# A planner that counts slow TensorE stretches and breaks up runs of row-maximum products and geometric scores

## What is computed

```python
q, k, v = heads(xn @ Wq), heads(xn @ Wk), heads(xn @ Wv)   # rope on q and k
scores = jnp.where(causal, jnp.einsum('bhtd,bhsd->bhts', q, k) * scale, NEG)
out = jax.nn.softmax(scores, axis=-1) @ v
geo = jnp.where(causal, qp[..., :, None] * kp[..., None, :], NEG)
geo_out = jax.nn.softmax(geo, axis=-1) @ v
out = out + scales * (geo_out - out)
x = x + out @ Wo + ffn(xn)    # top-102 of 1024 hidden units, ternary weights
```

## Time and profile before

| | us |
|---|---|
| median of three runs | 769.25 (768.81 to 769.69) |
| the profiled execution | 764.82 |
| its span, from the first to the last instruction | 762.7 |
| PE busy in it | 703.0 (92%) |
| DVE, ACT, POOL busy | 495.1, 449.3, 225.2 |
| mean granted TensorE clock | 0.924 of full speed |

### The profile page before, as it was taken

One profiled execution on the slowest core, in us unless ns is written; L12 is line 12 of the kernel. 1 busy time (PEld: TensorE's weight loads), 2 busy tenths in 40 slices (PEclk: granted clock), 3 DMA queues, 4 the chain that ended last, 5 costly groups with the idle time before them and its releaser, 6 DMA issues.

```text
span 762.7 us, 12315 instructions
## 1 busy us (share of the span) xinstructions
PE 703.0 (92%) x4424; PEld 328.5 (43%) x4424; DVE 495.1 (65%) x973; ACT 449.3 (59%) x733; POOL 225.2 (30%) x304
## 2 busy tenths in 40 slices
PE   4799898999799999998999999999999999998993
PEld 2443443434444442343344444464444465454532
DVE  5855987476568665667685876876567757467602
ACT  5434444444674533367554443679989998977550
POOL 4332336203222120133100121224432334266332
PEclk9866987989999998988999999999989999999997
DMA  8485000002700000052000000010000000000000
GB/s 244 171 229 138 10 8 1 28 1 63 206 9 2 1 1 1 3 135 62 1 6 1 1 1 1 10 33 31 15 28 29 23 22 29 9 22 8 1 1 28
DMA packets 26162, 30.74 MB, mean 40 GB/s; under 512 B 7089, under 2 KB 21297, under 8 KB 25714
## 3 DMA queue, kind: packets, MB, share of 16 engines
q1 hardware_dynamic: 24178, 29.38, 13.5%
q10 hardware_dynamic: 1920, 0.54, 0.3%
HBM read 17.72 MB, written 11.53 MB: 38 GB/s over the span
## 4 chain that ended last, share of the span: by engine, by line
PE 74%; DVE 9%; ACT 5%; issue 4%; DMA 3%; SPq 1%; POOL 1%; ACTq 0%; DVEq 0%; POOLq 0%
PE acc L1432 17%; PE acc L1425 16%; PE side L1324 11%; PE scores L1407 8%; PE scores L1411 4%; ACT probs L899 3%; DVE piece_max L1133 3%; PE side L1361 2%; PE side L1303 2%; PE side L1378 2%; PE side L1386 2%; PE side L1379 2%; PE side L1369 2%; PE side L1362 2%; DVE side L1136 1%
## 5 line engine op out<-in xcount | busy, mean ns | idle before, releaser
L899 ACT ACTIVATE probs<-scores 128x1024 f32<-128x1024 f32 (+3 forms) x320 | 270.3, 892 | 239.4 <-PE acc L1432 195.8
L1133 DVE TENSOR_REDUCE piece_max<-side 128x1 f32<-128x512 f32 x190 | 126.3, 686 | 76.2 <-PE side L1324 74.5
L1425 PE MATMUL acc<-probs,v_nat 128*32 128x512 f32 (+3 forms) x1280 | 161.6, 579 | 2.3 <-POOL probs L756 1.5
L1432 PE MATMUL acc<-probs,ones_all 128*32 128x512 f32 (+3 forms) x1280 | 158.6, 569 | 0.0
L1324 PE MATMUL side<-k_stack,q_stack 96*128 96x512 f32 (+3 forms) x315 | 125.0, 452 | 9.9 <-DVE piece_max L1133 2.8
L756 POOL TENSOR_SCALAR_AFFINE_SELECT probs<-probs 128x256 f32<-128x256 f32 x128 | 55.3, 439 | 238.0 <-ACT probs L899 236.6
L1324 PEld LDWEIGHTS side<-k_stack,q_stack 96*128 96x128 f32 x315 | 56.9, 200 | 104.8 <-issue 48.5
L1407 PE MATMUL scores<-q_stack,k_stack 98*128 98x512 f32 (+3 forms) x320 | 91.8, 392 | 4.2 <-ACT probs L899 4.0
L1136 DVE CUSTOM_DVE_ANT_0 side<-side,tail_mask 128x256 f32<-128x256 f32 (+3 forms) x125 | 61.3, 497 | 23.6 <-PE side L1324 23.0
L1425 PEld LDWEIGHTS acc<-probs,v_nat 128*32 128x32 f32 x1280 | 37.4, 115 | 80.1 <-issue 68.1
L1159 DVE RECIPROCAL d_raw<-d_raw 128x512 f32<-128x512 f32 x16 | 53.5, 3347 | 27.5 <-ACT o_raw L912 27.5
(11 more groups left out here) (163 smaller groups left out, 900.1 us busy)
## 6 DMA issues: line engine op xcount, KB each, us to landing
q_stack<-q_parked SPq DMA_DIRECT2D x12, 512.0 KB, 7.1
q_parked<-turned SPq DMA_DIRECT2D x8, 512.0 KB, 3.0
res<-in_L_attn_x_dram SPq DMA_DIRECT2D x4, 512.0 KB, 6.3
x_parked<-xn SPq DMA_DIRECT2D x4, 512.0 KB, 2.9
xT_parked<-xnT SPq DMA_DIRECT2D x4, 512.0 KB, 2.7
xz<-xT_parked SPq DMA_DIRECT2D x16, 128.0 KB, 2.5
xb<-x_parked SPq DMA_DIRECT2D x16, 128.0 KB, 2.0
out_dram<-res SPq DMA_DIRECT2D x16, 128.0 KB, 1.7
```

The lines of the kernel that those rows point to most:

```text
L899: nc.scalar.activation(probs[:, slot % 2, pair, :, off:], scores[:, pair, :, off:], ACT.Exp, scale=ATT_SCALE if kind == 0 else 1.0).then_i ...
L1133: free(nc.vector.tensor_reduce(piece_max[:, h, p:p + 1], pt, AX.X, ALU.max), ("S",) + a)
L1425: nc.tensor.matmul(acc[D * h:D * h + D, 0, off:], v_nat[:, j, g], probs[:, slot_no[a] % 2, h // 2, h % 2, off:], start=(j == 0), stop=(j = ...
L1432: last = nc.tensor.matmul(acc[D * h:D * h + D, 1, off:], ones[:, 0:D], probs[:, slot_no[a] % 2, h // 2, h % 2, off:], start=(j == 0), stop ...
```

## The change

The planner gets two additions. First, TensorE's clock in the plan no longer advances by an operation's length alone. `array` splits time into stretches of a fixed length, adds up in each the work done, weighted by kind (`WEIGHTS`: 0.72 for `S`, 0.77 for the usual scores, 0.14 for geometric ones, 0.06 for `gx`, 1 for the rest), and lets the next stretch run at half speed where that sum is under `ENOUGH`. These are numbers of the code, no measurements. Second, `thin` names the kinds geometric scores, `S`, `gx`, `found` and `wsum`; `idle_work` counts the time since the last operation of another kind. Where a thin operation would take it over `LIMIT` (1200 ns), another kind is taken if one can start within `PATIENCE` (900 ns) of it. No instruction is added or taken away on any engine, and none changes in size; only the orders change, and with them the banks.

```diff
--- before.py
+++ after.py
@@ -46,6 +46,13 @@
            "xnT_park": 3500, "khi_park": 2200, "klo_park": 2200, "hi_park": 3500, "lo_park": 3500, "stack_hi": 6000,
            "stack_lo": 4500, "xz_in": 2300, "xb_in": 2300}
 STAT_RANK = 3
+WINDOW = 3413.3
+PHASE = 0.0
+ENOUGH = 1500.0
+FULL = 1.0
+WEIGHTS = {"S": 0.72, "score0": 0.77, "score1": 0.14, "gx": 0.06, "found": 0.0, "wsum": 0.0}
+LIMIT = 1200
+PATIENCE = 900
 LEAD = 0.02
 REACH = 0.85
 Z_RANK = 11
@@ -262,8 +269,31 @@
         resting = at < len(keys) and any(d not in done for d in op[keys[at]][2])
         return range(BANKS + 2 * PAIRS) if key[1] == "S" and resting else range(BANKS)
 
+    worked = {}
+
+    def speed(n):
+        return 1.0 if worked.get(n - 1, 0.0) >= ENOUGH else 0.5
+
+    def array(key, at, ns):
+        weight = WEIGHTS.get(key[1] if key[0] == "unit" else key[0] + str(key[3]) if key[0] == "score" else key[0], 1.0)
+        left_ = ns
+        while left_ > 0:
+            n = int((at - PHASE) // WINDOW)
+            v = speed(n)
+            part = min(left_, (PHASE + (n + 1) * WINDOW - at) * v)
+            worked[n] = worked.get(n, 0.0) + part / v * weight * FULL
+            left_ -= part
+            at += part / v
+            if part < 1e-6:
+                at += 1e-3
+        return at
+
     clock = {e: 0.0 for e in ("pe", "dve", "act", "pool", "sp")}
+    def thin(key):
+        return key[0] == "score" and key[3] == 1 or key[0] == "unit" and key[1] in ("S", "gx", "found", "wsum")
+
     mode = "full"
+    idle_work = 0.0
     heads = {q: 0 for q in queue}
     plan = {e: [] for e in clock}
     landing = LANDING
@@ -308,7 +338,12 @@
         first = min(b[0] for b in best)
         close = [b for b in best if b[0] <= first + SLACK and b[3] == min(best)[3]]
         start, rank, key, eng, flow, ns, m = min(close, key=lambda b: (b[1], b[0]))
+        if eng == "pe" and thin(key) and idle_work + ns > LIMIT:
+            full_ = [b for b in best if b[3] == "pe" and not thin(b[2]) and b[0] <= start + PATIENCE]
+            if full_:
+                start, rank, key, eng, flow, ns, m = min(full_, key=lambda b: (b[0], b[1]))
         if eng == "pe":
+            idle_work = idle_work + ns + start - clock[eng] if thin(key) else 0.0
             mode = m
             if key[0] == "unit":
                 i = min((i for i in banks_for(key) if free_from(i) is not None), key=free_from)
@@ -317,7 +352,10 @@
             if key[0] == "score":
                 for i in range(2):
                     holds[BANKS + 2 * key[5] + i] = key
-        clock[eng] = start + ns
+        if eng == "pe":
+            clock[eng] = array(key, start, ns)
+        else:
+            clock[eng] = start + ns
         done[key] = clock[eng] + landing.get(key[0], 0)
         plan[eng].append(key)
         heads[(eng, flow)] += 1
```

## The result

| | before | after |
|---|---|---|
| median of 13 runs, us | 768.27 (761.70 to 773.25) | 776.29 (771.08 to 777.66) |
| profiled execution, us | 764.82 | 776.06 |
| its span | 762.7 | 774.0 |
| PE busy | 703.0 | 700.8 |
| span less PE busy | 59.7 | 73.2 |

The changed kernel is slower by 1%: ratio 1.0107, 95% interval 1.0080 to 1.0135. 774.8 was forecast, in a range of 758 to 787.

A forecast was written before the change was run, and what follows sets the result against it. The prediction took PE, busy 92% of the span, as the bound: its work, low clock and waits. Terms -11 + 3.6 - 2 + 5.5 + 2 + 6.5 + 1 = +5.6 us gave a median of 774.8 us, range 758 to 787.

The forecast's parts named there:

- The clock, -11: Behind 85 us: half-clock stretches behind thin runs go, gaining 11 us, ends 5 and 16.
- the seven stretches: Half-clock stretches at 120 to 482 us behind row-maximum products and geometric scores; 32.60 us of busy PE, all to go.
- The prediction's rival on the other side: Whole kernel: clock gain larger than the stalls, low stretch at 51.73 us also halved; 760 us, chance 0.34.
- Changes of neighbour, +3.6: PE's order throughout: 36 more borders between value steps and other kinds at 0.1 us each, +3.6 us.
- Small waits, -2: PE ahead of usual scores: alternating scores and values leave ACT more time for exponentials, -2 us, ends -4 and +1.
- Chunk 0, +5.5: From `mT` to first usual scores: reciprocal ahead of `m` on DVE makes PE wait 7.5 instead of 1.65 us.
- Chunk 2, +2: From `gx` to first `S`: PE waits 7.0 instead of 4.9 us, for the stack; +2 us, ends 0 and +4.
- Chunk 3, +6.5: From `gx` to first `S`: 7.1 us of work, PE waits 8.5 instead of 2.1 us; ends +3 and +8.5.
- Chunk 1, +1: Rope transposes now come soon after `gx` of chunk 1; +1 us, ends 0 and +2.5.
- those for right: 100-490 us: no full-load low stretches behind thin work; chunk 3 first-`S` wait 4 us or more; chunk 0 distance some 9 us.
- those for wrong: Chunk 3 first `S` unwaited or under 14 us after `gx`; clock near 0.924; exponential waits growing in last third.
- The rival with pauses alone as the cause of the low clock: Whole kernel: no low stretch goes, borders and stalls stay, +17 us; 786 us, chance 0.06.

The follow-up runs named there:

- the one from 79 us: Changed kernel with both additions acting only from the planner's 79 us on; 767.75 us, ratio 0.9984 to the kernel before.
- dense piece: Changed kernel with one unit of rope transposes near 72 us done five times over, same result; 779.86 us, ratio 1.0133 to the kernel before.
- the clock model with the right landings: Changed kernel with the limit out of reach and stack landings planned at 9.5 and 8.6 us; 769.14 us, ratio 1.0000 to the kernel before.
- right landings: Changed kernel with the planner's stack landings set to 9.5 and 8.6 us instead of 6 and 4.5; 760.44 us, ratio 0.9904 to the kernel before.
- the limit from 79 us: Changed kernel with the clock model throughout but the limit only from the planner's 79 us on; 770.71 us, ratio 1.0038 to the kernel before.
- the reciprocal moved: Kernel with landings 9.5 and 8.6 us, chunk 0's second geometric reciprocal put behind `m` and five reductions on DVE; 760.99 us, ratio 0.9895.
- the moved reciprocal: Changed kernel, old landings, chunk 0's second geometric reciprocal put behind `m` and the five reductions that follow on DVE; 779.85 us, ratio 1.0142.

## Why the prediction was right, and where it was not

The forecast was +5.6 us; the medians of 13 runs differ by 8.0, the profiled executions by 11.2. By the steps of the prediction:

- **The clock, -11: in effect -1.** Its first half held in the main. Of the seven stretches two have a successor, with 6.83 + 10.13 = 16.96 us of busy PE instead of 32.60 in the seven. In all, PE's busy time at half clock behind chunk 0's scores fell by 16.4 us, and that is -7.7 of the -11, inside the ends of 5 and 16. What failed is that the term was summed over the seven stretches behind 85 us as if the order ahead of them stayed as it was. Ahead of the scores of chunk 0 the clock cost 6.7 us more, by one execution of each kernel. The changed kernel and its copies with the same order on PE there have 39.2 to 43.9 us of busy time at half clock, the kernel before and the one from 79 us 29.7 to 35.8; so the cost lies between 1.6 and 6.7 us. The prediction's rival on the other side had even priced that place as a gain (-4.7), "since value steps now come between its thin runs earlier". The reverse was measured. From 66 to 84 us value steps come one and two at a time between `S`, scores and transposes, and the clock stayed at half; the first three in a row (84.94 to 89.44) are followed by full clock at 90.11, and in the other kernel one dense piece brought it back at once. The reading that fits is that breaking up thin runs with single value steps also breaks up the runs of value steps, and that it is these that bring the clock back. The dense piece supports it, but no run here puts the value steps of this stretch together and keeps the rest, so it is argued and not shown. The kernels with the limit from the start and the old landings have 50.6 to 56.2 us at half clock ahead of chunk 0's scores (limit alone 53.3, the changed kernel 52.9, and its edited copies but for the dense one, which has 43.1); those without the limit there have 34.1 to 41.0 (before and the clock model alone 34.1, both from 79 us and the clock model with the right landings 37.5, the limit from 79 us 41.0). With the right landings it is 38.0 in spite of the limit, and 34.8 with the reciprocal moved, so the limit is not a sufficient cause.
- **Changes of neighbour, +3.6: about 0.** PE's busy time from 30 us to the last `sum`, less 47% of that at half clock, is 679.09 - 46.5 = 632.6 before and 678.16 - 45.5 = 632.7 after. The 36 more borders left no trace in these sums. The price of the way back was taken as 0.1 us without a row; whether that or the price of leaving the value steps failed is not shown.
- **Small waits, -2: 0.** For exponentials PE waited 4.0 + 3.0 us before and 5.0 + 1.9 after; for the cuts of the triangle 1.5 and 4.1. So the step that failed is that scores and values that alternate more leave ACT more time: the wait that the term was about grew by 1.0 us. The wait for the triangle's cut, which comes behind ACT on the same path, grew by 2.6 and had no term. In the last third (500 us on) the waits for exponentials grew from 2.3 to 3.5 us and those for cuts from 1.0 to 2.7: the growth that the prediction named as left out.
- **Chunk 0, +5.5: +2.5, and nothing gained by taking it back.** PE waited 1.69 + 2.46 = 4.15 us between the transposed maxima and the scores, not 7.5, where it was 1.65. The distance was 7.98 us, not 9.5: the reciprocal did not wait for ACT's copy, contrary to the pattern of the earlier trace rows. And moving it back shortened the distance to 5.4 us without making the kernel faster, with either landing. DVE is the engine that is full there (10.20 of 10.55 us), and a place in its queue chooses who waits. Of the 14.1 us by which the scores were late, 11.8 lie ahead of the transposed maxima: 4.9 are clock (0.47 x (40.06 - 29.73)), and 6.3 are PE not busy (6.57 to 12.83). In these are 2.33 for the last row maximum and 6.0 for the transposes at 40.40 and 43.63, where it was 3.75. The longest wait, 4.76 us, is for two copies by ACT (`up_T`) that now stand behind its issue of six DMAs, 4.87 us long; one of them stood there before. The clock model alone has this wait too (4.9 us) and is the fastest kernel, so it is no sufficient cause of the loss either.
- **Chunk 2, +2: +2.1.** PE waited 7.0 us between `gx` and the first `S` (0.18, 0.20, 0.32 and 6.33) instead of 4.9. That is the forecast to a tenth, through the mechanism named: the stack is some 16 us away and the planner calls 8.6 us of work enough.
- **Chunk 3, +6.5: +3.1.** The waits are 0.88 + 0.65 + 0.18 + 0.32 + 3.17 = 5.2 us instead of 2.1. The distance was as worked out, 15.5 us. The work between was costed at full clock (7.1 us) and ran at half for 6.8 us of it; what PE did more slowly it did not wait for. The term that was to carry the sign has half its size, and the first `S` alone waited 3.17 us, not 4.
- **Chunk 1, +1: +0.4** (the wait ahead of 71.88 us).

The sum of the terms as measured is -1.1 + 0 + 0 + 2.5 + 2.1 + 3.1 + 0.4 = +7.0; the rest of the 11.2 is waits ahead of chunk 0's transposed maxima and for POOL, which had no term. So the number came out because a clock gain that was too large stood beside waits that were partly too large and partly left out; that it came so near is luck. The argument for the sign, stalls of known landing times against a clock gain of uncertain size, held. As a cause of what was measured it holds only in part: moving the first `S` alone won 2 us at chunk 3's maxima and nothing at the end.

By the prediction's own signs the mechanism did not pass. Of those for right, the low stretches at full load were not all gone (141.31, 281.26), the wait at chunk 3's first `S` was 3.17 us and not 4, and the distance in chunk 0 was 7.98 us and not 9. Of those for wrong, two came: the mean granted clock stayed near 0.924 (0.921), and the waits for exponentials in the last third grew.

The rival with pauses alone as the cause of the low clock fell. In the clock-only kernel, without an instruction added or taken away, PE is busy at half clock for 21 us less, though it stands still 4.2 us longer. In the changed kernel the clock fell at 281.26 us, and PE had been busy for 2.89 of the 2.97 us from 278.15 to 281.12; and it stayed low from 71.88 to 90.11 us while PE was busy for 18.13 of 18.23 us. By the Trainium skill (TensorE: Matmul & The Clock Gate, section "Why this matters for your kernels"), which puts the loss to idle gaps, neither should happen; the measurements decide, and they say that what PE runs counts as well.

That the clock's gain could be larger than the stalls, the rival at 760 us, is what the planner's clock model does when the limit leaves it alone: 758.78. It comes by another way than the rival's, since no thin run is broken up there by rule.

Open: why right landings help with the limit and hurt without it; 5.4 of the 15.6 us that they brought; and why the limit alone gets back most of its late chunk 0 and the changed kernel does not.

## What to carry to other kernels

Breaking up thin work on TensorE gave clock back behind chunk 0 (-7.7 us) and took it ahead (+6.7 at most); look at what ends a low stretch, not only at what starts it. When a planner's rule is changed, the whole order is drawn anew and moves the time by up to 16 us here, so a single wait is priced by moving its own entries and nothing else. Two additions to a planner are to be timed one at a time: one of these was worth -9.3 us, and the pair +8.

## What the runs showed of the hardware

The clock differs between executions with the same order and nearly the same times. The kernel with the dense piece and the changed kernel have the same order from 76 us on, and reach the transposed maxima of chunk 3 at 542.65 and 542.76 us. Then, the first in the kernel with the dense piece, the second in the changed one:

```profile
550.51:557.34 6.83, 6.31 (x26) 4.43 (x19) 4.88 (x7) 4.87 (x12) 0.00 (x0) 0.50 0.08 23
```

```profile
550.51:557.34 6.83, 5.68 (x38) 3.86 (x34) 6.33 (x13) 5.85 (x16) 0.01 (x1) 1.00 0.08 23
```

26 matmul instructions at half clock in the one, 38 at full clock in the other, 0.1 us apart at the start. A stretch like that is worth 3 us. A kernel's runs spread by several of them, 761.7 to 773.3 us for the kernel before, and their time goes with the mean granted clock: in 23 runs of it on one chip the fastest took 762.60 us at 0.926 and, at the lowest clock, one took 773.27 us at 0.909. As an estimate, 0.017 less of 765 us is 26 us more at half clock, and 0.47 x 26 = 12 us; 10.7 were measured. The two fastest kernels, the clock model alone and the right landings, spread over 2 us only (758.04 to 760.03, 759.96 to 761.58). A single profile can't tell a loss of 3 us by an edit from such a stretch; the medians of the moved reciprocal and of the dense piece, each 3.6 us over the changed kernel, stand under the same doubt, since their intervals overlap its own.
